# Context mixing of a two-layer decoder: from two programs over the whole stage to one program by batches

## The chip, the cores and the metric

The kernel runs on one core of a Trainium2 chip. The metric is device microseconds from launch to end, as the median of repeated runs. One further execution is recorded by the hardware profiler; all rows below are of that one.

## The reference

A decoder of two layers works on x, four batches of 512 tokens by 512 features. Each sublayer adds to x. The change lies in the second sublayer of layer 0, "context mixing", which follows an attention with 16 heads and stands ahead of a packed feed-forward net:

```
x = x + attention(layernorm(x))                      # layer 0 attention
x = x + context_mixing(layernorm(x), ctx, Wq, bq, Wk, bk)
x = x + packed_ffn(layernorm(x)); ...                # and layer 1

def context_mixing(xn, ctx, Wq, bq, Wk, bk):         # ctx: 4 x 512 x 256; Wq, Wk: 128 x 256
    query, key = ctx @ Wq.T + bq, ctx @ Wk.T + bk    # 4 x 512 x 128
    energy = query @ key.T                           # 4 x 512 x 512
    attention = softmax(energy)
    return xn @ attention.T                          # mixes the 512 features
```

The attention matrix depends on the context alone; x enters only in the last product.

## The kernel before, in words

x stays in on-chip memory as `x_res`, 16 tiles of 128 tokens by 512 features, 4 tiles to a batch. The decoder is a row of stages, each ended by a barrier of all engines. Every matrix product is made of three passes: each operand is split into a high and a low half (`_hi`, `_lo`), and high·high, high·low and low·high are summed. A tile that must lie the other way round is turned by TensorE (four 128x128 transposes into one 512-column bank, below a "turn"). ScalarE then copies the high half out of the bank, and VectorE takes the low half, which frees the bank.

`layer0_attention` projects queries and keys, stores them to device memory, and then attends over 32 pairs of heads. SyncE's queue loads pair after pair (`att.loads`, six pairs ahead).

`feature_attention` is the stage of the change. It holds two programs, one after the other.

The first, `load_context` with `norm_to_features`, loads the context (2 MB), the two weights and the two biases in one wave, and TensorE waits for all of them. VectorE meanwhile makes the statistics of all 16 tiles of x (`bn_stats`, L158). Then 8 turns of context and 2 of weights follow, the chain of small operations L163 to L171 with a square root on ScalarE (L232), and 16 turns of normalised x, through a ring of four `xn` buffers, into `xT_hi` and `xT_lo` for all four batches.

The second is the mixing. The banks are two `work`, four of `energy` and two `turn`. By batch b: `project_qk` makes query and key (12 matmuls, L1107), ScalarE and VectorE split them (L1157, L1180), `energies` makes 4 x 3 matmuls (L1116), VectorE takes the row maxima (L1188), ScalarE the exponentials (L1162), VectorE inverts the sums and scales the rows (L1195, L1198), `turn_attention` turns the 4 tiles (L1126, L1170, L1212), and `mix` makes four groups of 12 matmuls (L1137), each added to x by VectorE (L1204). The order of the work of each engine is written out by hand. For batch b TensorE does turn_attention(b), project_qk(b+1), energies(b+1), mix(b), so the softmax of the next batch lies beside the mixing.

`Ring` and `Norm` exist already and serve layer 0's attention: `Ring` is a list of turns through a few banks (a turn waits until the low half was taken of the job that had its bank before), `Norm` makes the statistics, the root and the scaling for one group of tiles.

Of the kernel before, what the change touches and what calls it, by code (L numbers as in the profile page):

```python
# [16 lines left out]
P = 128  # L17
F32 = mybir.dt.float32
# [12 lines left out]
T = B * QT  # L31
# [48 lines left out]
def setup(st, x_in):  # L80
    st.x_in = x_in

# [692 lines left out]
def layer0_attention(st, Wq_w, Wq_b, Wk_w, Wk_b, Wv_w, Wv_b):  # L775
# [4 lines left out]
    k_dram = nc.dram_tensor("l0_k", (2, HD, TOK), F32).ap()  # L780
    with ExitStack() as stack:
# [3 lines left out]
        wT_hi = sb("l0_wT_hi", [P, KC, D + 2 * HD], F32R)  # L785
        wT_lo = sb("l0_wT_lo", [P, KC, D + 2 * HD], F32R)
# [32 lines left out]
        k_stored = st.sem("k_stored")  # L819
# [232 lines left out]
def feature_attention(st, ctx_in, Wq, bq, Wk, bk):  # L1052

# [3 lines left out]
    with ExitStack() as stack:  # L1057
        sb, ps = tensors(nc, stack)
        features(st, stack, "fa")
# [5 lines left out]
        with ExitStack() as loading:  # L1065
            sb2, _ = tensors(nc, loading)
            raw = sb2("fa_w", [P, 2, C], F32)
            loads = [(raw[:, 0, :], Wq), (raw[:, 1, :], Wk), (bias[:, 0:1], column(bq)), (bias[:, 1:2], column(bk))]
            jobs = [([raw[:, n, c * P:(c + 1) * P] for n in range(2)], wT_hi[:, c, :], wT_lo[:, c, :])
                    for c in range(CC)]  # L1070
# [4 lines left out]
        prob = sb("fa_prob", [P, QT, S], F32)  # L1075
# [6 lines left out]
        energy = ps("fa_energy", [P, QT, S])  # L1082
        turn = [ps(f"fa_turn{n}", [P, 512]) for n in range(2)]
        worked, work_read, hi_done, scored, nmax_ready, exp_done, rden_done, prob_ready, turned, att_hi, turn_read = \
            st.sems("worked", "work_read", "hi_done", "scored", "nmax_ready", "exp_done", "rden_done", "prob_ready",
                    "turned", "att_hi", "turn_read")

# [8 lines left out]
        with nc.Block() as block:  # L1096

            @block.tensor
            def _(pe):
                def project_qk(b):  # L1100
                    for n in range(2):
                        if b:
                            pe.wait_ge(work_read, qk_use(b, n) - 1)
                        m = 0
                        for c in range(CC):
                            for w, x in ((wT_hi, ctxT_hi), (wT_hi, ctxT_lo), (wT_lo, ctxT_hi)):
                                last = pe.matmul(work[n][:], w[:, c, n * P:(n + 1) * P], x[:, c, b * S:(b + 1) * S],  # L1107
                                                 start=(m == 0), stop=(m == 3 * CC - 1))
                                m += 1
                        last.then_inc(worked, 1)  # L1110

                def energies(b):
                    pe.wait_ge(work_read, qk_use(b, 1) + 1)
                    for q in range(QT):
                        for m, (qq, kk) in enumerate(((hi[0], hi[1]), (hi[0], lo[1]), (lo[0], hi[1]))):
                            last = pe.matmul(energy[:, q, :], qq[:, q * P:(q + 1) * P], kk[:], start=(m == 0),  # L1116
                                             stop=(m == 2))
                        last.then_inc(scored, 1)

                def turn_attention(b):  # L1120
                    pe.wait_ge(prob_ready, b + 1)
                    for k in range(QT):
                        if QT * b + k >= 2:
# [1453 lines left out]
```

## Time and profile before

| what | us |
|---|---|
| median of 3 runs (2779.58 to 2780.4) | 2779.88 |
| the profiled execution's own time | 2776.81 |
| its span, first to last instruction | 2775.1 |
| layer 0 attention ends at | 375.6 |
| last addition of the mixing starts at | 514.07 |

Over the span TensorE's matmuls are busy 2493.5 us (90%), its weight loads 1808.0 (65%), VectorE 1750.2 (63%), ScalarE 1199.2 (43%). TensorE's matmuls overlap their neighbours, so a busy share of 90% does not say that TensorE is at its peak. In a timeline, the first column is the start, the second the duration, and the bracket at the end says how long the engine sat idle ahead of the row and what released it. A row of busy time by stretches gives the stretch, its length, the busy time with the number of instructions of TensorE's matmuls (PE), its weight loads (PEld), VectorE (DVE), ScalarE (ACT) and GpSimd (POOL), then TensorE's granted clock as a share of full speed, the share of the DMA engines and GB/s. A group of instructions gives busy time, mean ns of one, then the idle time ahead of them.

### The profile page before, as it was taken

Reading aid. Unit: us, or ns where it says so; the run is one execution under the profiler, and the core shown is the slowest. Engines: PE = TensorE matmul, PEld = TensorE weight load, DVE = VectorE, ACT = ScalarE, POOL = GpSimd, SP = SyncE. Lnnn points to the kernel's source line nnn. Section 1 sums busy time; section 2 is a strip of 40 time slices with the busy share of each in tenths; the row PEclk is TensorE's granted clock in tenths of the full one; section 3 lists DMA queues with packets and bytes.
Section 4 is the critical chain, followed back from the end, with each engine's and each line's share of the span. In section 5 each row is a group of like instructions: output and inputs, shape, how many; then the busy total and the mean of one; then the engine's idle time right before and its main releaser. Section 6 shows DMA issues by size and latency. Waiting matters only on the chain. (4 is left out here: it accounts for less than half of the span.)

```text
span 2775.1 us, 39696 instructions
## 1 busy us (share of the span) xinstructions
PE 2493.5 (90%) x11524; PEld 1808.0 (65%) x11524; DVE 1750.2 (63%) x3675; ACT 1199.2 (43%) x2342; POOL 157.6 (6%) x263
## 2 busy tenths in 40 slices
PE   7999968679999939989999689999999999999579
PEld 5555536557777727744445567777777777777457
DVE  6677765567777572256664657666666666767643
ACT  3566643223333232246664244444444444444321
POOL 0000000000000000010003011010100101010000
PEclk9999989779999979989999899999999999999789
DMA  5422110000000023343330100000000000000101
GB/s 166 129 69 68 48 34 0 17 1 1 0 0 0 1 65 121 118 117 89 84 78 0 32 30 12 11 15 4 15 11 8 11 11 15 4 8 0 39 1 61
DMA packets 71459, 103.69 MB, mean 37 GB/s; under 512 B 14447, under 2 KB 27514, under 8 KB 71262
## 3 DMA queue, kind: packets, MB, share of 16 engines
q1 hardware_dynamic: 71390, 102.82, 12.5%
q8 instruction: 37, 0.61, 0.1%
q14 instruction: 32, 0.26, 0.0%
HBM read 72.90 MB, written 29.88 MB: 37 GB/s over the span
## 5 line engine op out<-in xcount | busy, mean ns | idle before, releaser
L2470 DVE SCALAR_TENSOR_TENSOR x_res<-xa_out_bank,xa_den,x_res 128x512 f32 (+1 forms) x256 | 191.4, 748 | 158.5 <-PE xa_out_bank L2110 158.5
L2379 ACT ACTIVATE xa_pT_hi<-xa_t_bank 128x512 fp32r<-128x512 f32 x256 | 149.7, 598 | 125.8 <-PE xa_t_bank L2247 125.8
L2390 ACT ACTIVATE xa_prob<-xa_prob,xa_nmax 128x512 f32<-128x512 f32 x256 | 182.7, 716 | 30.0 <-DVE xa_nmax L2452 30.0
L2110 PE MATMUL xa_out_bank<-xa_o_w,xa_o_hi 128*128 128x512 f32 x512 | 172.8, 419 | 24.3 <-DVE x_res L2470 22.9
L2434 DVE TENSOR_TENSOR xa_pT_lo<-xa_t_bank,xa_pT_hi 128x512 fp32r<-128x512 f32 x256 | 175.8, 687 | 23.3 <-ACT xa_pT_hi L2379 19.3
L2452 DVE CUSTOM_DVE_ANT_0 xa_prob<-xa_s_bank,xa_mask_bias 128x512 f32<-128x512 f32 x256 | 171.1, 687 | 19.9 <-PE xa_s_bank L2110 9.5
L1535 DVE TENSOR_TENSOR ffn_y<-ffn_y 128x512 f32<-128x512 f32 x176 | 120.4, 689 | 70.5 <-PE ffn_y L1355 68.3
L581 DVE TENSOR_REDUCE l1s_mx<-l1s_max_bank 128x1 f32<-128x512 f32 x256 | 156.2, 681 | 12.7 <-PE l1s_max_bank L443 12.6
L581 DVE TENSOR_REDUCE l0s_mx<-l0s_max_bank 128x1 f32<-128x512 f32 x256 | 156.0, 681 | 2.8 <-PE l0s_max_bank L443 2.7
L2247 PE MATMUL xa_t_bank<-ident,xa_prob 128*128 128x128 f32 x1024 | 150.6, 275 | 0.0
L2247 PEld LDWEIGHTS xa_t_bank<-ident,xa_prob 128*128 128x128 f32 x1024 | 121.1, 141 | 39.6 <-issue 18.1
L568 ACT ACTIVATE l1s_pT<-l1s_score_bank 128x512 f32<-128x512 f32 x256 | 139.8, 601 | 15.3 <-PE l1s_score_bank L462 14.0
L568 ACT ACTIVATE l0s_pT<-l0s_score_bank 128x512 f32<-128x512 f32 x256 | 138.9, 601 | 9.1 <-PE l0s_score_bank L462 8.5
L443 PE MATMUL l1s_max_bank<-l1s_k,l1s_q 96*128 96x512 f32 x256 | 118.7, 473 | 16.6 <-DMA l1s_k<-l_k 8.4
L2371 ACT ACTIVATE xa_q_hi<-xa_bank_a 128x512 fp32r<-128x512 f32 x64 | 38.4, 600 | 197.5 <-PE xa_bank_a L2220 197.5
L2110 PEld LDWEIGHTS xa_out_bank<-xa_o_w,xa_o_hi 128*128 128x128 f32 x512 | 84.9, 190 | 59.2 <-issue 44.4
L472 PE MATMUL l1s_o_bank<-l1s_pT,l1s_vs 128*64 128x512 f32 x512 | 118.4, 605 | 0.0
L472 PE MATMUL l0s_o_bank<-l0s_pT,l0s_vs 128*64 128x512 f32 x512 | 116.9, 598 | 0.0
L443 PE MATMUL l0s_max_bank<-l0s_k,l0s_q 96*128 96x512 f32 x256 | 114.4, 451 | 2.2 <-DVE l0s_mx L581 1.6
L2259 PE MATMUL xa_o_bank<-xa_pT_hi,xa_v_hi 128*128 128x512 f32 x256 | 108.7, 425 | 0.1
L2110 PE MATMUL xa_s_bank<-xa_k_hi,xa_q_hi 128*128 128x512 f32 x256 | 106.4, 416 | 2.3 <-DVE xa_q_lo L2434 2.0
L462 PE MATMUL l1s_score_bank<-l1s_q,l1s_k 98*128 98x512 f32 x256 | 103.1, 406 | 1.8 <-ACT l1s_pT L568 1.1
(418 smaller groups left out, 5981.1 us busy)
## 6 DMA issues: line engine op xcount, KB each, us to landing
l0s_q<-l_q SPq DMA_DIRECT2D x96, 128.0 KB, 2.4
l1s_q<-l_q SPq DMA_DIRECT2D x96, 128.0 KB, 3.2
l1s_k<-l_k SPq DMA_DIRECT2D x96, 128.0 KB, 3.4
l0s_k<-l_k SPq DMA_DIRECT2D x96, 64.0 KB, 2.4
x_res<-in_x_dram SPq DMA_DIRECT2D x4, 1024.0 KB, 9.9
l_q<-l_q_hi SPq DMA_DIRECT2D x16, 256.0 KB, 2.7
l_q<-l_q_lo SPq DMA_DIRECT2D x16, 256.0 KB, 3.3
l_q<-l1p_hi SPq DMA_DIRECT2D x16, 256.0 KB, 2.1
```

What stands on the lines that cost most here:

```text
L443: pe.matmul(self.max_bank[(2 * s + j) % 3][:], self.qs[s][0:self.STK, n, q * P:(q + 1) * P], self.ks[s][0:self.STK, n % self.KN, :], start ...
L472: last = pe.matmul(self.o_bank[self.W * n:self.W * (n + 1), :], self.vs[s % 2][:, kt, n, :], self.pT[:, n, kt, :], start=(kt == 0), stop=( ...
L568: act.activation(self.pT[:, n, kt, :], self.score_bank[(2 * s + k) % 3][:], ACT.Exp, scale=HD ** -0.5)\
L581: dve.tensor_reduce(self.mx[:, j // QT, j % QT:j % QT + 1], self.max_bank[(2 * s + j) % 3][:], AX.X, ALU.max)\
L1535: dve.tensor_tensor(yt, y_bank[t % 2][:], yt, ALU.add).then_inc(y_read, 1)
L2110: last = pe.matmul(bank, w, x, start=(m == 0), stop=(m == len(pairs) - 1))
L2247: last = pe.transpose(t_bank[kt % 2][:, q * P:(q + 1) * P], prob[:, q, kt * P:(kt + 1) * P], st.ident[:])
L2379: act.activation(pT_hi[:, kt % (QT - 1), :], t_bank[kt % 2][:], ACT.Copy).then_inc(pT_hi_done, 1)
L2390: act.activation(prob[:, q, :], prob[:, q, :], ACT.Exp, bias=nmax[:, q:q + 1], scale=-1.0, accum_out=den[:, r, 0, q:q + 1]).then_inc(exp_d ...
L2434: dve.tensor_tensor(lo, bank, hi.bitcast(F32), ALU.subtract).then_inc(lo_done, 1)
L2452: dve.tensor_tensor_reduce(prob[:, q, :], s_bank[q % 2][:], mask_bias[:], -scale, -LOW * 1e-5, ALU.add, ALU.min, nmax[:, q:q + 1]).then_in ...
L2470: dve.scalar_tensor_tensor(xt, out_bank[:], den[:, r, 2, q:q + 1], xt, ALU.mult, ALU.add)\
```

## The change

The two programs of `feature_attention` become one, by batches.

1. Context and weights are loaded by `layer0_attention` (now `project_and_attend`), on SyncE's queue behind the last stores of projections and ahead of `att.loads`, into the room of layer 0's projection weights. The biases are loaded in the mixing program.
2. All turns (weights, context, x, attention) go through one `Ring` with three banks. `energy` has three banks in place of four, `work` still two. The context of batch b+2 is turned in the middle of mix(b).
3. x is normalised by batches with `Norm`: statistics, root and scaling of batch b+1 lie beside the work of batch b. Its turned form exists for one batch at a time.
4. The scaling of the softmax's rows moves from VectorE to ScalarE, and `prob` has two buffers.

```
 layer 0 attention, SyncE
+                sp.wait_ge(projected, NF * B)
+                sp.dma_start(st.fa_raw[0], ctx_in.rearrange("b (q p) c -> p (b q) c", p=P)).then_inc(fa_loaded, 16)
+                for n, w in enumerate((fa_Wq, fa_Wk)):
+                    sp.dma_start(st.fa_raw[1][:, n, :], w).then_inc(fa_loaded, 16)
                 att.loads(sp)
+                sp.wait_ge(fa_loaded, 48)
...
-            load_context(st, ctx_in, ctxT_hi, ctxT_lo, loads, jobs, "fa_prep")
+        norm = Norm(st, stack, "fan", [t[:] for t in xn])
-        energy = ps("fa_energy", [P, QT, S])
-        turn = [ps(f"fa_turn{n}", [P, 512]) for n in range(2)]
+        energy = [ps(f"fa_energy{n}", [P, S]) for n in range(3)]
+        turn = [ps(f"fa_turn{n}", [P, 512]) for n in range(3)]
+        ring = Ring(st, "far", turn, jobs)
...
 TensorE
+                def energies(b, q):
+                    if q == 0:
+                        pe.wait_ge(work_read, qk_use(b, 1) + 1)
+                    reached(pe, exp_done, QT * b + q - 2)
...
-                project_qk(0)
-                energies(0)
+                for c in range(CC):
+                    ring.turn(pe, at["w", c])
+                turn_context(0)
+                for n in range(2):
+                    project_qk(0, n)
+                turn_context(1)
+                for q in range(QT):
+                    energies(0, q)
                 for b in range(B):
-                    turn_attention(b)
-                    if b < B - 1:
-                        project_qk(b + 1)
-                        energies(b + 1)
+                    more = b + 1 < B
+                    for q in range(3):
+                        turn_x(b, q)
+                    if more:
+                        project_qk(b + 1, 0)
+                    turn_x(b, 3)
+                    turn_attention(b, 0)
+                    if more:
+                        project_qk(b + 1, 1)
+                    turn_attention(b, 1)
+                    turn_attention(b, 2)
+                    if more:
+                        energies(b + 1, 0)
+                    turn_attention(b, 3)
+                    if more:
+                        for q in range(1, QT):
+                            energies(b + 1, q)
                     for t in range(QT):
                         mix(b, t)
+                        if t == 1 and b + 2 < B:
+                            turn_context(b + 2)
...
 ScalarE
+                norm.root(act, 0, batch_tiles(0))
+                for c in range(CC):
+                    ring.take_hi(act, at["w", c])
+                take_context(0)
+                for n in range(2):
+                    take_qk(0, n)
+                take_context(1)
                 exponentials(0)
+                normalise(0)
                 for b in range(B):
+                    more = b + 1 < B
+                    for q in range(3):
+                        ring.take_hi(act, at["x", b, q])
+                    if more:
+                        take_qk(b + 1, 0)
+                    ring.take_hi(act, at["x", b, 3])
+                    ring.take_hi(act, at["a", b, 0])
+                    if more:
+                        take_qk(b + 1, 1)
+                    for k in range(1, QT):
+                        ring.take_hi(act, at["a", b, k])
+                    if more:
+                        norm.root(act, b + 1, batch_tiles(b + 1))
                         exponentials(b + 1)
+                        normalise(b + 1)
+                    if b + 2 < B:
+                        take_context(b + 2)
...
 VectorE
+                norm.stats(dve, 0, batch_tiles(0))
...
                 maxima(0)
                 normalise(0)
+                invert(0)
                 for b in range(B):
...
+                    for k in range(1, QT):
+                        ring.take_lo(dve, at["a", b, k])
+                    if more:
+                        norm.stats(dve, b + 1, batch_tiles(b + 1))
                         maxima(b + 1)
+                        add(b, 0)
+                        invert(b + 1)
+                        add(b, 1)
+                        if b + 2 < B:
+                            take_context(b + 2)
                         normalise(b + 1)
+                        add(b, 2)
+                        add(b, 3)
```

In the new program `normalise` on VectorE scales x (`Norm.normalise`), and `normalise` on ScalarE scales the four rows of `prob`. VectorE's order in the part that is left out is ScalarE's: each low half follows its high half.

## Rows read from the trace of the kernel before

**Rows 1.** Busy time by stretches: the stage of the change.

```profile
375.70:515.90 140.20, 102.75 (x452) 81.00 (x452) 80.66 (x142) 43.49 (x85) 0.00 (x0) 0.87 0.06 17
```

**Rows 2.** Timeline of all engines, start of the stage and its last addition.

```profile
377.00 0.40 SPq L101 DMA_DIRECT2D fa_prep_ctx<-in_ctx_dram  x1
377.34 9.59 DVE L158 BATCH_NORM_STATS2 fa_prep_bn<-x_res  x16 [1.71 <-PEq L57]
386.54 6.16 PEld L117 LDWEIGHTS fa_prep_w_bank<-ident,fa_prep_ctx 128*128 128x128 f32 x32 [12.31 <-DMA fa_bias<-in_L_xattn_bk_dram]
...
514.07 0.69 DVE L1204 TENSOR_TENSOR x_res<-fa_work,x_res 128x512 f32<-128x512 f32 x1 [2.10 <-PE fa_work L1137]
```

**Rows 3.** Groups of instructions by line and shape, stretch 376 to 516.

```profile
L1162 ACT ACTIVATE fa_prob<-fa_energy,fa_nmax 128x512 f32<-128x512 f32 x16 | 10.8, 686 | 9.2 <-DVE fa_nmax L1188 9.2
L1212 DVE TENSOR_TENSOR fa_attT_lo<-fa_turn,fa_attT_hi 128x512 fp32r<-128x512 f32 x16 | 10.5, 688 | 6.2 <-ACT fa_attT_hi L1170 6.2
L1180 DVE SCALAR_TENSOR_TENSOR fa_lo<-fa_work,fa_bias,fa_hi 128x512 fp32r<-128x512 f32 x8 | 6.0, 752 | 10.6 <-ACT fa_hi L1157 10.6
L1157 ACT ACTIVATE fa_hi<-fa_work,fa_bias 128x512 fp32r<-128x512 f32 x8 | 5.5, 688 | 11.2 <-PE fa_work L1107 11.2
```

**Rows 4.** Busy time by stretches: turning part of batch 1, turning and mixing of batch 3.

```profile
453.00:463.10 10.10, 7.56 (x40) 5.84 (x39) 6.20 (x10) 4.37 (x9) 0.00 (x0) 1.00 0.00 0
496.20:501.00 4.80, 2.46 (x18) 1.72 (x16) 3.27 (x5) 2.28 (x4) 0.00 (x0) 1.00 0.00 0
501.00:514.80 13.80, 12.98 (x48) 10.08 (x48) 2.77 (x4) 0.00 (x0) 0.00 (x0) 0.88 0.00 0
```

**Rows 5.** Timeline of TensorE: first projection; batch 1's turns and first mixing matmul; batch 2's turns.

```profile
416.46 0.77 PE L1107 MATMUL fa_work<-fa_ctxT_hi,fa_wT_hi 128*128 128x512 f32 x1 [2.00 <-PEq L190]
...
453.00 1.04 PE L1126 MATMUL fa_turn<-ident,fa_prob 128*128 128x128 f32 x8
...
463.49 0.39 PE L1137 MATMUL fa_work<-fa_attT_hi,fa_xT_hi 128*128 128x512 f32 x1
...
474.68 1.03 PE L1126 MATMUL fa_turn<-ident,fa_prob 128*128 128x128 f32 x8
```

**Rows 6.** Busy time by stretches: after the first softmax's idle time.

```profile
425.40:429.00 3.60, 0.09 (x1) 0.09 (x2) 2.58 (x7) 1.54 (x6) 0.00 (x0) 1.00 0.00 0
429.00:431.00 2.00, 1.25 (x9) 0.85 (x9) 0.76 (x2) 1.19 (x2) 0.00 (x0) 0.66 0.00 0
```

**Rows 7.** Timeline of VectorE in layer 0's projection: statistics of one batch by `Norm`.

```profile
20.30 2.47 DVE L745 BATCH_NORM_STATS2 l0n_bn<-x_res 128x6 f32<-128x512 f32 x4
23.80 0.16 DVE L753 SCALAR_TENSOR_TENSOR l0n_mv<-l0n_mv 128x4 f32<-128x4 f32 x1
25.73 1.92 DVE L767 TENSOR_SCALAR l0s_pT<-x_res,l0n_mv 128x512 f32<-128x512 f32 x4
```

**Rows 8.** Timeline of ScalarE: table loads, in layer 0 and in the mixing.

```profile
73.55 1.28 ACT L970 ACT_TABLE_LOAD   x1
74.84 0.20 ACT L970 ACTIVATE l0s_warm<-ident 128x1 f32<-128x1 f32 x1
...
421.56 1.28 ACT L1162 ACT_TABLE_LOAD   x1
424.11 0.69 ACT L1162 ACTIVATE fa_prob<-fa_energy,fa_nmax 128x512 f32<-128x512 f32 x1 [1.27 <-DVE fa_nmax L1188]
```

**Rows 9.** Timeline of TensorE: batch 1's projections and first energy, at half clock.

```profile
432.60 0.78 PE L1107 MATMUL fa_work<-fa_ctxT_hi,fa_wT_hi 128*128 128x512 f32 x1
...
438.96 0.50 PE L1116 MATMUL fa_energy<-fa_hi 128*128 128x512 f32 x1 [1.56 <-DVE fa_lo L1180]
```

**Rows 10.** Groups of ScalarE's instructions: one that reads and writes on-chip memory.

```profile
L1428 ACT ACTIVATE ffn_h_hi<-ffn_h 128x512 fp32r<-128x512 f32 x44 | 27.8, 633 | 139.8 <-DVE ffn_h L1525 139.8
```

**Rows 11.** Timeline of SyncE's queue at the end of the projections.

```profile
94.25 0.43 SPq L850 DMA_DIRECT2D l_q<-l_q_lo  x1
102.82 0.38 SPq L416 DMA_DIRECT2D l0s_q<-l_q  x1
```

More of the change, by code:

```diff
@@ L780, in layer0_attention @@
     k_dram = nc.dram_tensor("l0_k", (2, HD, TOK), F32).ap()
+    NW = D + 2 * HD
+    st.carried = ExitStack()
+    with ExitStack() as under:
+        wT_hi, wT_lo = (sb_tensor(nc, under, f"l0_wT_{part}", [P, KC, NW], F32R) for part in ("hi", "lo"))
+    later = sb_tensor(nc, st.carried, "fa_raw", [P, 2 * KC * NW])
+    st.fa_raw = (later[:, 0:T * C].rearrange("p (t c) -> p t c", t=T),
+                 later[:, T * C:T * C + 2 * C].rearrange("p (n c) -> p n c", n=2))
+    ctx_in, fa_Wq, fa_Wk = st.fa_inputs
     with ExitStack() as stack:
@@ L1096, in feature_attention, with _ @@
         with nc.Block() as block:
+            @block.sync
+            def _(sp):
+                for n, vec in enumerate((bq, bk)):
+                    sp.dma_start(bias[:, n:n + 1], column(vec), allow_slow_non_contiguous=True).then_inc(b_loaded, 16)
+                sp.wait_ge(b_loaded, 32)
             @block.tensor
             def _(pe):
[L1100 to L1123, printed above, removed]
-                            pe.wait_ge(turn_read, QT * b + k - 1)
-                        for q in range(QT):
-                            last = pe.transpose(turn[k % 2][:, q * P:(q + 1) * P], prob[:, q, k * P:(k + 1) * P],
-                                                st.ident[:])
-                        last.then_inc(turned, 1)
+                def project_qk(b, n):
+                    u = qk_use(b, n)
+                    reached(pe, work_read, u - 1)
+                    pe.wait_ge(ring.lo_done, at["c", b, CC - 1] + 1)
+                    m = 0
+                    for c in range(CC):
+                        for w, x in ((wT_hi, ctxT_hi), (wT_hi, ctxT_lo), (wT_lo, ctxT_hi)):
+                            last = pe.matmul(work[n][:], w[:, c, n * P:(n + 1) * P], x[:, c, b * S:(b + 1) * S],
+                                             start=(m == 0), stop=(m == 3 * CC - 1))
+                            m += 1
+                    last.then_inc(worked, 1)
@@ new lines, in energies @@
+                def energies(b, q):
+                    if q == 0:
+                        pe.wait_ge(work_read, qk_use(b, 1) + 1)
+                    reached(pe, exp_done, QT * b + q - 2)
+                    for m, (qq, kk) in enumerate(((hi[0], hi[1]), (hi[0], lo[1]), (lo[0], hi[1]))):
+                        last = pe.matmul(energy[(QT * b + q) % 3][:], qq[:, q * P:(q + 1) * P], kk[:], start=(m == 0),
+                                         stop=(m == 2))
+                    last.then_inc(scored, 1)
@@ L1166, in _, with take_context @@
+                def take_context(b):
+                    for c in range(CC):
+                        ring.take_hi(act, at["c", b, c])
+                norm.root(act, 0, batch_tiles(0))
+                for c in range(CC):
+                    ring.take_hi(act, at["w", c])
[3 more added lines that the diff above has]
+                take_context(1)
                 exponentials(0)
+                normalise(0)
                 for b in range(B):
-                    for k in range(QT):
-                        act.wait_ge(turned, QT * b + k + 1)
-                        act.activation(attT_hi[:, k, :], turn[k % 2][:], ACT.Copy).then_inc(att_hi, 1)
```

150 lines of the change are left out of this document (97 added, 53 removed).

## The prediction

> **What bounds the kernel now.** I read the busy time by stretches first. The stage lasts 140.2 us, from 375.7 to 515.9; TensorE is busy 102.75 us of it at a mean granted clock of 0.87, VectorE 80.66, ScalarE 43.49 [rows 1]. No engine is full, so the order of the work sets the time.
>
> The timeline then shows two halves. VectorE starts at 377.34 with 16 statistics (9.59 us). TensorE waits 12.3 us, until 386.54, for the last of five loads issued from 377.00 on [rows 2]. Ten turns of context and weights, the chain with the root and 16 turns of x follow, until the first projection at 416.46 [rows 5]. From there one batch costs 21.7 us: the turns of batch 1 start at 453.00 and those of batch 2 at 474.68. Of this 48 mixing matmuls take 474.68 − 463.49 = 11.2 us, 0.233 each [rows 5]. The turning part ahead of them (attention turns, projections, energies) lasts 10.1 us with TensorE busy 7.56, at full clock [rows 4]. So the old stage is 39 us of preparation and start, and 98 us of batches and their ends.
>
> **The change part by part.** One turn costs TensorE 0.42 us (two last 1.04 with the tail of the last [rows 5]), at half clock 4 x 6.16/32 = 0.77 [rows 2]. The high half then costs ScalarE 0.60 and the low half VectorE 0.69 [rows 3]. A matmul's result comes 0.2 us behind its slot (it lasts 0.39 [rows 5]). Handing over between engines costs 0.03 to 0.06, which I put into the sums.
>
> *The loads.* The three move to SyncE's queue in layer 0. The last store ahead is issued at 94.25 and the first reload of a pair at 102.82 [rows 11]. Even if the queue were held for the whole 9.5 us that all five loads take [rows 2], the first reload would come at 104.2, 1.4 us late. It brings pair 6, needed four pairs on, at (375.6 − 100)/32 = 8.6 us a pair. Cost 0; the attention beside it is the cover. The biases are two issues at the new program's start, needed some 10 us later: 0.
>
> *The start, new.* 377.3: statistics of four tiles and their chain, 3.67 us (20.30 to 23.96 [rows 7]). The root is first on ScalarE's queue and holds the high halves behind it until 381.2. Two weight halves (each about 0.4) and the two contexts of batch 0, the second one waiting for a bank and turned at half clock: 384.7. Two projections to the first energy: 6.4 us, as 432.60 to 438.96 [rows 9], since TensorE sat nearly idle: 390.9. Four energies, maxima and exponentials: with three banks the fourth energy waits for the first exponential. First maximum at 392.0, first exponential 392.7 to 393.4, fourth energy until 394.3, its maximum until 395.05. VectorE then scales four tiles of x (two small ones and 1.92 [rows 7]) before it inverts the sums: 397.5. ScalarE scales four rows at 0.6 to 0.63 (the nearest row reads and writes on-chip memory in 0.633 [rows 10]): 400.0. Only then does it take the turned x.
>
> *One batch's turning part.* From the first turn of x, TensorE's order makes this chain: three turns 1.26, first projection 1.40, two turns 0.84, second projection 1.40 plus 0.2, ScalarE takes the key 0.69, VectorE 0.75 [rows 3], first energy at 6.6, last attention turn until 7.3, to ScalarE 0.63, high 0.60, low 0.69: 9.3 us. Eleven of VectorE's pieces fit in (7.7 us), as do ScalarE's (6.2).
>
> *The new stall.* After the last turn TensorE has energies 1 and 2, done at 9.15, and then energy 3, which wants the bank of energy 0, so its exponential. Behind energy 3 in the queue stands the whole mixing. VectorE's order puts the next batch's statistics ahead of its maxima: 9.3 + 3.67 = 13.0. ScalarE does the root (13.2) and must then load the exponential's table, 1.28 [rows 8]: 14.5; exponential 0.69: 15.2. Energy 3 takes 0.7, and mixing starts at 15.9. TensorE idles 6.1 us in each of three batches.
>
> *The mixing.* 11.2 us and two context turns 0.84: the batch ends at 28.0 at full clock, against 21.7 before. VectorE's additions, invert, context halves and scaling of x end before it (by my count at 27.2), so they cost nothing; if TensorE were 1 us faster here they would not either.
>
> *The clock.* In rows 6 TensorE goes idle at 425.4, and the granted clock, 1.00 until 429.0, is 0.50 soon after. My stall is longer, so the work behind it starts at half speed (1.2 GHz). What that costs shows at 501.0 to 514.8: clock 0.88 [rows 4], so 0.12 x 13.8 = 1.66 us. I take 1.65 for each batch. The last batch has no projections; its eight turns are a ring of three banks with 2.0 us a round, 0.67 each, 6.65 in all. TensorE is 50% busy there, as at 496.2 to 501.0 (2.46 of 4.8), after which the clock did fall: 1.65 again.
>
> **The sum.** Start to batch 0's mixing: 400.0, plus 8.65 (the turning part from ScalarE's first x on), plus 0.6 for a projection that I expect at half clock (full it is 0, wholly half 5), plus 6.6 for statistics to mixing: 415.9. Batch 0: 11.2 + 0.84 + 1.65 = 429.6. Batch 1: 28.0 + 1.65 = 459.2. Batch 2, without context turns: 28.8, 488.0. Batch 3: 6.65 + 11.2 + 1.65 and 0.9 for the last addition: 508.4. Before, that addition ends at 514.07 + 0.69 = 514.8 [rows 2]. The gain is 6.4 us: the profiled execution goes from 2776.8 to 2770.4. Its own time is 3.1 below the median shown, so against the median I say 2779.9 − 6.4 = 2773.5. The stages behind begin as before. Thus the wins (loads and most of the preparation, about 39 us up to the first projection) are nearly given back by four longer turning parts and three stalls.
>
> A rule that speaks against the change is that of the Trainium skill, "ScalarE: Activation LUTs", section "What ACT_TABLE_LOAD costs": a switch of table sets costs 2.66 us, 1.28 of load and 1.38 of drain. The trace does not bear out the second part: the load of 73.55 ends at 74.83 and the next activation starts at 74.84 [rows 8]. By the rule the sum would be some 1.38 worse at each of four exposed switches; it is rival C, priced below from a row.
>
> **The rivals.**
> A: the clock does not fall. For it: the whole turning part of batch 1 stayed at 1.00 with TensorE 75% busy [rows 4]. Against it: the 6.1 us without work. Four times 1.65 would come back, and the 0.6: 2766.3.
> B, the other side: the turning parts run at half clock. Turns were at 0.50 to 0.66 from 429 on [rows 6] and at 386 [rows 2]. The chain of 9.3 then becomes three turns 2.3, projection 2.6, two turns 1.5, projection 2.6 and tail 0.4, key 1.5, energy 1.3, turn 1.1, halves 1.3: 14.6, and energy 3 costs 0.6 more, 5.9 a batch. A single batch uses up 5.9 of the 6.4; from the second on the kernel is slower. All three: 2791. Against it: the part is 90% busy until the stall and follows a dense mixing.
> C: a table load has a drain behind it. For it: 1.27 us idle between the end of the load (422.84) and the exponential at 424.11 [rows 8]; against it: that exponential's maximum ended only just before, and 74.84. Four exposed switches at 1.27: 5.1, so 2778.6, no change that can be told.
> D: the hiding is worse than drawn: banks and handovers that come late in the start and at each batch, 1 us for each of four turning parts and 2 in the start, 2779.5. The context load would be part of it if it held up the pairs.
>
> **How the numbers follow.** Forecast 58 in 100, A 16, B 8, C 6, D 12. A measurement of this kernel tells 0.2% (5.6 us, 2774.3) from no change. The forecast's own range is 2770 to 2777; it lies at the border, so of its 58 I count 38 as faster and 20 as no change. Faster: 38 and A, 54. No change: 20, C and 11 of D, 37. Slower: B and 1 of D, 9. The range reaches from A to past D: 2765 to 2782.
>
> **What would show it.** After: no load at the stage's head, first turn's high half near 381.2, first mixing matmul near 416. TensorE idle about 6 us ahead of the fourth energy of batches 1 to 3, released by ScalarE's exponential, with a 1.28 us table load ahead of it. Mixing to mixing near 29 us. Granted clock half for some 3.5 us behind each stall. The last addition ends near 508. I am wrong if the mixing starts without that wait, if the clock stays at 1.00 (then 2766), if turns and projections ahead of the stall show half clock, or if layer 0's end moves from 375.6.

## The result, and the profile after

| | before | after |
|---|---|---|
| median, us | 2780.4 (20 runs, 2775.18 to 2785.11) | 2774.35 (20 runs, 2770.94 to 2777.44) |
| profiled execution, us | 2776.81 | 2776.7 |
| layer 0 attention ends at | 375.63 | 379.83 |
| first statistics of the stage start at | 377.34 | 381.26 |
| last addition of the mixing ends at | 514.76 | 512.85 |
| stage, statistics to last addition | 137.42 | 131.59 |

The changed kernel takes 0.9978 of the time before (95% interval 0.9971 to 0.9984), 6.05 us less. The forecast was 6.4 less, and 2773.5 us for the median. At 0.22% the gain lies just above the 0.2% that the prediction counts as told from no change, and its interval reaches down to 0.16%. The two profiled executions hardly differ, because the one of before lies at the low end of its runs and the one of after above its median. So the readings below compare lengths: the stage is 137.42 − 131.59 = 5.8 us shorter. "The stage" is always that stretch here, unless a start is named. All instants of the prediction shift by 381.26 − 377.34 = 3.92 us, and what is left is the error. The two ends of the stage, in VectorE's timeline, after:

```profile
381.26 2.47 DVE L749 BATCH_NORM_STATS2 fan_bn<-x_res 128x6 f32<-128x512 f32 x4 [1.43 <-PEq L57]
...
512.16 0.69 DVE L1305 TENSOR_TENSOR x_res<-fa_work,x_res 128x512 f32<-128x512 f32 x1 [2.12 <-PE fa_work L1188]
```

Busy time of the whole stage, after. The row answers to [rows 1]:

```profile
379.90:514.30 134.40, 98.89 (x452) 77.65 (x452) 75.30 (x150) 60.33 (x111) 0.00 (x0) 0.87 0.00 1
```

TensorE runs the same 452 matmuls at the same mean clock of 0.87, and it is still busy only 98.89 of 134.40 us. Its idle time was 140.20 − 102.75 = 37.5 us and is 35.5. The head of the stage with its loads and 16 turns of x is gone; the idle time has moved.

Timeline of all engines from the start to batch 0's softmax, after (rows left out between them):

```profile
384.96 0.21 ACT L762 ACTIVATE fan_mv<-fan_mv 128x4 f32<-128x4 f32 x1 [2.46 <-DVE fan_mv L757]
385.07 0.64 ACT L720 ACTIVATE fa_wT_hi<-fa_turn 128x256 fp32r<-128x256 f32 x2
...
388.48 0.79 PE L1154 MATMUL fa_work<-fa_ctxT_hi,fa_wT_hi 128*128 128x512 f32 x1 [1.41 <-DVE fa_ctxT_lo L725]
...
394.79 0.50 PE L1164 MATMUL fa_energy<-fa_hi 128*128 128x512 f32 x1 [0.76 <-DVE fa_lo L1280]
...
399.41 1.91 DVE L771 TENSOR_SCALAR fa_xn<-x_res,fan_mv 128x512 f32<-128x512 f32 x4
...
401.44 2.57 ACT L1241 ACTIVATE fa_prob<-fa_prob,fa_rden 128x512 f32<-128x512 f32 x4 [1.53 <-DVE fa_rden L1293]
...
405.36 0.75 PE L709 MATMUL fa_turn<-ident,fa_xn 128*128 128x128 f32 x4 [2.39 <-DVE fa_xT_lo L725]
```

The root stands first on ScalarE's queue, and the high half of the first weights follows it at 385.07, though TensorE had turned the weights from 381.26 on. ScalarE scales four rows in 2.57 us, and the first turned x is taken only behind that. The fourth turn of x waits 2.39 us for the bank that this holds.

Timeline of all engines around the first stall, after:

```profile
413.07 1.28 ACT L762 ACT_TABLE_LOAD   x1
413.08 0.69 DVE L725 TENSOR_TENSOR fa_attT_lo<-fa_turn,fa_attT_hi 128x512 fp32r<-128x512 f32 x1 [0.93 <-ACT fa_attT_hi L720]
413.69 2.46 DVE L749 BATCH_NORM_STATS2 fan_bn<-x_res 128x6 f32<-128x512 f32 x4
...
417.18 0.16 DVE L757 SCALAR_TENSOR_TENSOR fan_mv<-fan_mv 128x4 f32<-128x4 f32 x1
417.27 1.89 DVE L1287 TENSOR_REDUCE fa_nmax<-fa_energy 128x1 f32<-128x512 f32 x3
417.38 0.21 ACT L762 ACTIVATE fan_mv<-fan_mv 128x4 f32<-128x4 f32 x1 [3.02 <-DVE fan_mv L757]
417.60 1.28 ACT L1235 ACT_TABLE_LOAD   x1
418.90 0.69 ACT L1235 ACTIVATE fa_prob<-fa_energy,fa_nmax 128x512 f32<-128x512 f32 x1
...
419.73 0.79 PE L1164 MATMUL fa_energy<-fa_hi 128*128 128x512 f32 x1 [5.92 <-ACT fa_prob L1235]
```

This is the chain that the prediction drew. Statistics (3.65 us), root, table load and exponential lie one behind another, while three finished energies wait for their maxima and TensorE waits for a bank. The exponential starts 418.90 − 417.60 − 1.28 = 0.02 us behind the end of its table's load.

The waits of TensorE in the stage (380 to 514), after: us in total, times, the longest. The row shown is the largest:

```profile
PE fa_energy L1164 <- ACT fa_prob L1235: 18.0, 4, 5.9
```

Busy time by stretches across that stall, after. They answer to [rows 6]; the clock is the third figure from the end:

```profile
413.00:415.00 2.00, 0.81 (x4) 0.33 (x2) 1.92 (x4) 1.34 (x2) 0.00 (x0) 1.00 0.00 0
415.00:417.00 2.00, 0.00 (x0) 0.00 (x0) 1.83 (x7) 0.00 (x0) 0.00 (x0) 0.74 0.00 0
417.00:419.00 2.00, 0.00 (x0) 0.00 (x0) 1.97 (x5) 1.59 (x3) 0.00 (x0) 0.50 0.00 0
...
421.00:425.00 4.00, 4.00 (x15) 3.13 (x15) 0.77 (x2) 0.80 (x3) 0.00 (x0) 0.78 0.01 4
```

The clock falls to 0.50 (1.2 GHz) while TensorE is idle, and the fourth energy and the first mixing matmuls run at that level. A turning part stays at 1.00 throughout (434 to 445, with TensorE busy 8.81 of 11 us, and 464 to 475 at 1.00 too).

Timeline of TensorE, after: the first turns of batches 1, 2 and 3, and batch 3's first mixing matmul. They answer to [rows 5]:

```profile
434.03 1.47 PE L709 MATMUL fa_turn<-ident,fa_xn 128*128 128x128 f32 x12
...
464.20 1.47 PE L709 MATMUL fa_turn<-ident,fa_xn 128*128 128x128 f32 x12
...
493.75 1.47 PE L709 MATMUL fa_turn<-ident,fa_xn 128*128 128x128 f32 x12
...
500.63 0.50 PE L1188 MATMUL fa_work<-fa_attT_hi,fa_xT_hi 128*128 128x512 f32 x1 [1.41 <-DVE fa_attT_lo L725]
```

From these, the stage against the prediction's sum:

| term | predicted | measured |
|---|---|---|
| start to the end of batch 0's mixing | 429.6 − 377.3 = 52.3 | 434.03 − 381.26 = 52.8 |
| batch 1 | 29.6 | 464.20 − 434.03 = 30.2 |
| batch 2 | 28.8 | 493.75 − 464.20 = 29.55 |
| batch 3, to the last addition's end | 20.4 | 512.85 − 493.75 = 19.1 |
| stage | 131.1 | 131.6 |

### The profile page after: what moved, and what is told of

It is laid out like the page before. It is cut to its first block and busy times, and to the rows that moved or that the text cites. A ratio compares the mean times of both kernels' runs of the same rounds, so it can differ in the third digit from the quotient of the medians.

```text
span 2775.0 us, 39683 instructions
## 1 busy us (share of the span) xinstructions
PE 2494.6 (90%) x11524; PEld 1807.2 (65%) x11524; DVE 1742.8 (63%) x3683; ACT 1218.0 (44%) x2367; POOL 157.4 (6%) x263
## 3 DMA queue, kind: packets, MB, share of 16 engines
q1 hardware_dynamic: 71390, 102.82, 12.5%
## 5 line engine op out<-in xcount | busy, mean ns | idle before, releaser
L2236 PE MATMUL xa_out_bank<-xa_o_w,xa_o_hi 128*128 128x512 f32 x512 | 173.3, 420 | 22.4 <-DVE x_res L2596 20.9
L572 ACT ACTIVATE l0s_pT<-l0s_score_bank 128x512 f32<-128x512 f32 x256 | 139.1, 603 | 10.9 <-PE l0s_score_bank L466 9.7
L2236 PE MATMUL xa_s_bank<-xa_k_hi,xa_q_hi 128*128 128x512 f32 x256 | 106.3, 415 | 2.2 <-DVE xa_q_lo L2560 2.0
```

The costliest lines, as they stand in the source:

```text
L572: act.activation(self.pT[:, n, kt, :], self.score_bank[(2 * s + k) % 3][:], ACT.Exp, scale=HD ** -0.5)\
L2236: last = pe.matmul(bank, w, x, start=(m == 0), stop=(m == len(pairs) - 1))
```

## The experiments

The stages of several experiments are compared in their profiles, since the executions of one kernel spread over 6.5 us (the changed one) to 9.9 us (the one before). Each median stands beside that of the kernel before, run on the same chip at the same time. Where an experiment ran beside the changed kernel too, that is said. Otherwise the two are compared by what each is below the kernel before, and that is 6.05 and 7.41 us for the changed kernel in its two series.

**The changed kernel again.** No edit.

> The changed kernel once more, for a second profile beside the variants. Theory: the stage (first instruction of the mixing program to the end of its last addition) again lasts 131.6 us, with three stalls of 5.9 us ahead of the fourth energy. Of layer 0's attention, which ended 4.2 us later in the one profile of after than in that of before (379.8 against 375.6) with a granted clock of 0.5 to 0.66 between 98 and 106 us: theory 1, the clock falls there by chance, so this profile can show either end; rival, the context load beside it brings it about, so it ends near 379.8 or at least 2.6 us late again.

Measured: 2774.7 us (10 runs) against 2782.11, ratio 0.997 (0.996 to 0.9979). The stage lasts 131.2 us. Layer 0's attention ends at 380.87, late again, so this run alone doesn't tell the theory from its rival; the next two do.

**The loads back into the stage.** Only part 1 of the change is undone (the lines are shortened):

```
 layer 0 attention, SyncE
-                sp.dma_start(st.fa_raw[0], ctx_in...)      # and Wq, Wk
                 att.loads(sp)
-                sp.wait_ge(fa_loaded, 48)
 mixing program, SyncE, ahead of the biases
+                sp.dma_start(ctx_raw, fa_in...)            # and Wq, Wk
 TensorE, ahead of the first turn
+                pe.wait_ge(fa_loaded, 48)
```

> The loads of context and weights go back into the mixing program, ahead of all else, with TensorE waiting for the three. Everything else stays as in the changed kernel. Theory: TensorE's first turn comes some 9.5 us after the issue instead of at once, of which 3.9 were covered by the first statistics: 6.3 us slower than the changed kernel, about the time of before. Rival, the load beside the attention costs 2.6 us or more there (see after_again): then the attention ends at 375.6 and only 3.7 us are lost.

Measured: 2782.51 us (10 runs), ratio 0.9996 (0.9986 to 1.0006) against the kernel before; 7.8 us above the changed kernel beside it. The stage is 138.27 us, 6.7 to 7.1 longer. It starts at 382.04, and TensorE's first turn waits for the last of the loads:

```profile
391.06 2.82 PE L709 MATMUL fa_turn<-ident,fa_raw 128*128 128x128 f32 x12 [11.60 <-DMA fa_raw<-in_L_xattn_Wk_dram]
```

The first projection comes 395.29 − 382.04 = 13.25 us behind the start in place of 7.22. So in this program the early load is worth as much as the whole gain, and the other three parts without it leave the time where it was. What an early load alone would give the kernel before was not run.

The experiment also bears on the test that the prediction failed: "if layer 0's end moves from 375.6". It did move, to 379.83. If the 2 MB beside the attention caused that, this kernel, which doesn't load them there, should end it at 375.6. It ends at 380.62.

**The kernel before, once more.** No edit, one execution.

> The kernel before once more, for a second profile. Eight profiles of variants show layer 0's attention ending between 376.7 and 380.9 with clock dips near 98 us and near 372 us, with the context load beside it or without; only the one profile of before shows 375.6 and no dip. Theory 1 (chance of the clock): this profile may show a dip as well, and in any case its stage from the end of the attention to the last addition lasts 139.1 us again, within 1. Rival (something of the changed kernel other than the load slows the attention): it ends at 375.6 again, without a dip.

Measured: 2784.46 us. Layer 0's attention ends at 378.70, 3.1 us later than in the first profile of the same kernel. From that end to the last addition it is 139.4 us (139.1 in the first profile). Busy time and granted clock near the start of the attention, in the order first profile of before, after, before once more, loads back:

```profile
97.00:105.00 8.00, 7.59 (x34) 3.67 (x36) 6.62 (x14) 5.73 (x10) 0.00 (x0) 1.00 0.07 26
```

```profile
97.00:105.00 8.00, 7.72 (x23) 4.73 (x24) 6.84 (x14) 4.48 (x8) 0.00 (x0) 0.60 0.77 250
```

```profile
97.00:105.00 8.00, 8.00 (x26) 5.51 (x28) 6.73 (x14) 5.08 (x9) 0.00 (x0) 0.62 0.01 2
```

```profile
97.00:105.00 8.00, 7.54 (x21) 4.60 (x21) 6.88 (x14) 4.11 (x7) 0.00 (x0) 0.64 0.07 26
```

The last three have the dip at 97 to 105, with 250 GB/s of loads or with 2 to 26. In the first profile of before the clock is 1.00 there. So the late end needs no load beside the attention. Nor does the load force it: in the nine profiles of kernels that have it there, the attention ends anywhere from 376.3 to 380.9. What is left is the clock, whose dips differ between executions of one kernel. That they make the end late is argued from their coming together, since no run forces a dip.

SyncE's queue in the changed kernel, which answers to [rows 11]:

```profile
94.47 0.43 SPq L860 DMA_DIRECT2D l_q<-l_q_lo  x1
97.78 0.39 SPq L871 DMA_DIRECT2D fa_raw<-in_ctx_dram  x1
98.22 3.05 SPq L873 DMA_DIRECT2D fa_raw<-in_L_xattn_Wq_dram  x1
101.32 0.49 SPq L873 DMA_DIRECT2D fa_raw<-in_L_xattn_Wk_dram  x1
105.08 0.37 SPq L420 DMA_DIRECT2D l0s_q<-l_q  x1
```

The three issues hold the queue until 101.8. The first reload comes at 105.08, 2.3 us later than before. But it stands 0.54 us behind the start of the first pair's output product (104.54), as it did before (102.82 behind 102.28) and does with the loads put back (105.63 behind 105.10). So it waited for the pair and not for the queue. The profile shows no wait of TensorE for a transfer during the whole attention.

**The stall filled with matmuls, in two amounts.** To price the clock apart from the wait, the third energy of batches 1 to 3 is computed N times over, 3 matmuls each time. The work fills idle time and moves nothing else:

```
-                    for m, (qq, kk) in enumerate(...):
-                        last = pe.matmul(energy[...][:], ...)
+                    for again in range(N if b and q == 2 else 1):
+                        for m, (qq, kk) in enumerate(...):
+                            last = pe.matmul(energy[...][:], ...)
```

N = 6:

> The third energy of batches 1 to 3 is computed six times over on the same operands instead of once, 5 x 0.70 = 3.5 us of idle TensorE filled per stall, nothing taken away. My term of the clock: the stall is idle for 2.5 us instead of 5.9, the clock stays at full speed, and each of three mixings saves 1.65 us: 5.0 us faster than the changed kernel. Rival (the slow start of the mixing has another cause than the idle time, or the 1.65 is covered): no change, or slower if the repeats delay the maxima.

N = 9:

> As e_warm, but the third energy is computed nine times over, which fills 5.6 of the 5.9 us of a stall and leaves TensorE about 0.4 us idle ahead of the fourth energy. In e_warm 2.5 us were left idle, the clock still fell in it, and only 0.3 us a batch came back. Theory (the clock falls because of the idle time ahead of the mixing): the fourth energy and the mixing now run at full clock from their start, 1.65 us saved in each of three batches less what the repeats delay: 4 to 5 us faster than the changed kernel. Rival (repeats of the same product do not count, or the drop has another cause): within 1.5 us of e_warm.

Measured, N = 6: 2773.46 us (5 runs), 1.2 under the changed kernel beside it, and no difference that can be told; 5.0 were expected. N = 9: 2768.27 us (4 runs), ratio 0.9949 (0.9932 to 0.9965); the changed kernel stood at 0.9978 and 0.997. Its stage is 126.09 us, 5.1 to 5.5 less, where 4 to 5 were expected. Busy time by stretches across the first stall, and then TensorE's timeline at its end, N = 6:

```profile
417.00:419.00 2.00, 0.00 (x0) 0.00 (x0) 1.54 (x3) 1.99 (x4) 0.00 (x0) 0.89 0.00 0
419.00:421.00 2.00, 1.89 (x5) 1.51 (x6) 0.21 (x1) 1.39 (x5) 0.00 (x0) 0.50 0.03 8
```

```profile
419.11 0.79 PE L1165 MATMUL fa_energy<-fa_hi 128*128 128x512 f32 x1 [2.51 <-ACT fa_prob L1236]
```

and both for N = 9:

```profile
417.00:419.00 2.00, 1.51 (x8) 0.93 (x7) 0.93 (x2) 1.99 (x6) 0.00 (x0) 1.00 0.00 0
419.00:421.00 2.00, 2.00 (x10) 1.64 (x9) 0.69 (x1) 1.48 (x5) 0.00 (x0) 1.00 0.04 8
```

```profile
418.41 0.50 PE L1165 MATMUL fa_energy<-fa_hi 128*128 128x512 f32 x1 [0.48 <-ACT fa_prob L1236]
```

With 2.51 us left idle the clock fell all the same, and the first matmul behind it took 0.79 us. In the next two stalls of that kernel the fourth energy still ran at full speed and the clock fell to 0.50 just behind it. With 0.48 left it stayed at 1.00 and the matmul took 0.50. In the second case the second batch takes 28.33 us in place of 30.2. From the fourth energy to the next batch's first turn the changed kernel takes 14.30, 14.76 and 14.12 us in the three batches with a stall, and this one 12.91, 12.93 and 12.03. So the clock's price is 1.4, 1.8 and 2.1 us, 5.3 in all. The 6-fold case failed as a test of that price, because it didn't keep the clock; the expectation had taken for granted that it would. The other 5.9 us of each stall stay in both kernels, as the exponential comes no sooner.

**The fourth energy behind half of the mixing.** The instruction that waits for the bank is put where TensorE has independent work ahead of it. VectorE's order follows:

```
 TensorE
-                        for q in range(1, QT):
+                        for q in range(1, QT - 1):
                             energies(b + 1, q)
                     for t in range(QT):
                         mix(b, t)
+                        if t == 1 and more:
+                            energies(b + 1, QT - 1)
 VectorE
-                        maxima(b + 1)
+                        maxima(b + 1, range(QT - 1))
                         add(b, 0)
+                        maxima(b + 1, range(QT - 1, QT))
+                        add(b, 1)
                         invert(b + 1)
-                        add(b, 1)
-                        if b + 2 < B:
-                            take_context(b + 2)
                         normalise(b + 1)
                         add(b, 2)
+                        if b + 2 < B:
+                            take_context(b + 2)
                         add(b, 3)
```

> The fourth energy of the next batch moves behind the second mixing group, VectorE takes its maximum behind the first addition. My account of the batch (9.3 turning, 6.6 from statistics to mixing, 12.0 mixing, 1.65 clock) says that mixing then starts at 9.35 and a batch lasts 22.5 instead of 29.6 to 30.2: three times 7.1 to 7.6, 21 to 23 us faster than the changed kernel. Rival: statistics, maxima and table load bound the batch on VectorE and ScalarE anyway (the next batch's maxima come late, and the next turning part waits for them); then a third of that or less, under 8 us.

Measured: 2749.89 us (4 runs), ratio 0.9884 (0.9868 to 0.9901), 24.8 below the changed kernel beside it. The stage lasts 109.23 us, 22.0 to 22.4 less, and a batch 22.66; 21 to 23 less was expected. The other 2.4 us or more of the medians' difference lie outside the stage and were not traced. Timeline of all engines at the same place, and busy time of the stretch:

```profile
414.06 1.89 DVE L1289 TENSOR_REDUCE fa_nmax<-fa_energy 128x1 f32<-128x512 f32 x3
...
414.40 1.28 ACT L1237 ACT_TABLE_LOAD   x1
...
415.87 0.68 DVE L1307 TENSOR_TENSOR x_res<-fa_work,x_res 128x512 f32<-128x512 f32 x1
...
416.53 0.50 PE L1164 MATMUL fa_energy<-fa_hi 128*128 128x512 f32 x1
```

```profile
413.00:425.00 12.00, 11.97 (x61) 9.63 (x61) 9.57 (x23) 8.47 (x18) 0.00 (x0) 1.00 0.01 1
```

Statistics, root and table load are as long as before. But TensorE is mixing beside them: the fourth energy has no idle time ahead of it, TensorE is busy 11.97 of 12 us, and the clock stays at 1.00. The waits of TensorE for `fa_prob` fall from 18.0 us to 0.3. The stalls and their clock made 3 x 5.9 + 5.3 = 23 us, which is near the 22 found. A fourth bank for `energy` would be another cure; it was not tried.

**Statistics and root one batch ahead.** TensorE's order is left as it is, and the work between the last energy and the exponential is taken away:

```
 VectorE, batch 1's statistics behind batch 0's softmax; in the loop
-                        norm.stats(dve, b + 1, batch_tiles(b + 1))
                         maxima(b + 1)
                         add(b, 0)
                         invert(b + 1)
+                        if b + 2 < B:
+                            norm.stats(dve, b + 2, batch_tiles(b + 2))
 ScalarE, batch 1's root behind normalise(0); in the loop
-                        norm.root(act, b + 1, batch_tiles(b + 1))
                         exponentials(b + 1)
                         normalise(b + 1)
                     if b + 2 < B:
                         take_context(b + 2)
+                        norm.root(act, b + 2, batch_tiles(b + 2))
```

> Statistics and root of x move one batch ahead (the statistics of batch b+2 behind the inversion of batch b+1, their root behind the context's high halves); nothing else is moved, the fourth energy stays ahead of the mixing. By my account the stall is 3.67 of statistics, 0.25 of root, 1.28 of table load, 0.69 exponential: with the first two gone and the table load hidden behind VectorE's last low half, it shrinks from 5.9 to about 1.6 us, so 4.3 a batch and the clock's 1.65, three times, less 1.4 at the start where statistics 1 and their table load now hold up the first x: 13 to 17 us faster than the changed kernel. Rival (the table load is the stall's core, or the statistics push the additions behind the mixing): under 7 us.

Measured: 2757.02 us (4 runs), ratio 0.9909 (0.9893 to 0.9926). The stage lasts 115.08 us, 16.1 to 16.5 less, where 13 to 17 were expected. The median is 25.5 below the kernel before, so 18 to 19 better than the changed kernel. The table load and the fourth energy of batch 1:

```profile
414.51 1.28 ACT L1235 ACT_TABLE_LOAD   x1
415.85 0.69 ACT L1235 ACTIVATE fa_prob<-fa_energy,fa_nmax 128x512 f32<-128x512 f32 x1
...
416.68 0.50 PE L1164 MATMUL fa_energy<-fa_hi 128*128 128x512 f32 x1 [1.43 <-ACT fa_prob L1235]
```

The stall is 1.43 us in place of 5.92, and the energy runs at full clock. So 4.5 us of each stall lay between ScalarE's last high half and the table load of the exponential: in the changed kernel that load waits for VectorE's last low half (413.08 on), the statistics (3.65) and the root (0.2), and starts 417.60 − 411.02 = 6.6 us behind the first energy. Here it starts 414.51 − 412.46 = 2.05 behind it. The start grew by 2.3 us (the first energy of batch 1 comes 32.1 us behind the start in place of 29.8). The parts add up: 3 x 4.5 + 5.3 − 2.3 = 16.5. This is the second, independent way to the same cause.

**Invert ahead of the scaling of x.** In the start VectorE inverts the sums ahead of scaling x, so that ScalarE comes free sooner:

```
                 maxima(0)
-                normalise(0)
                 invert(0)
+                normalise(0)
```

> One swap at the start: VectorE inverts the sums of batch 0 before it scales x, not behind it. ScalarE's scaling of the four rows then starts when the last exponential is done, some 1.4 us sooner, and the first high half of x with it. Theory: 1.0 to 1.5 us faster than the changed kernel, all of it ahead of the first addition. Rival: the scaled x comes later by as much and the turns wait for it: no change.

Measured: 2769.96 us (4 runs, 2768.39 to 2775.28), ratio 0.9954 (0.9938 to 0.9971). By the median that is 5 to 6.5 us better than the changed kernel, more than the 1.0 to 1.5 expected; in the profile, whose own time of 2775.28 is the highest of the four, the stage is 133.47 us, 1.9 longer. Busy time of the same stretches in this kernel and, in the second fence, in the changed one:

```profile
400.00:403.00 3.00, 2.09 (x10) 2.10 (x11) 2.15 (x7) 2.96 (x6) 0.00 (x0) 0.53 0.01 3
403.00:407.00 4.00, 4.00 (x15) 3.31 (x14) 1.97 (x3) 1.84 (x4) 0.00 (x0) 0.50 0.00 0
```

```profile
400.00:403.00 3.00, 2.96 (x18) 2.28 (x18) 1.41 (x4) 1.56 (x3) 0.00 (x0) 1.00 0.01 3
403.00:407.00 4.00, 1.64 (x9) 1.50 (x10) 2.48 (x5) 3.63 (x7) 0.00 (x0) 0.84 0.00 0
```

ScalarE did take the first x sooner, by 0.5 us from the start (22.16 against 22.65), but in that execution the first turns and projections ran at 0.53 and 0.50. What the edit is worth by itself stays open; the three executions of 2768.4 to 2771.5 left no profile.

**All together.** Late fourth energy, invert first, and batch 0's statistics and root moved behind the first context and the first query:

```
 VectorE
-                norm.stats(dve, 0, batch_tiles(0))
                 for c in range(CC):
                     ring.take_lo(dve, at["w", c])
                 take_context(0)
+                norm.stats(dve, 0, batch_tiles(0))
 ScalarE
-                norm.root(act, 0, batch_tiles(0))
...
                 for n in range(2):
                     take_qk(0, n)
+                    if n == 0:
+                        norm.root(act, 0, batch_tiles(0))
```

> e_late and e_invert together, and at the start the root of batch 0 behind ScalarE's first query instead of ahead of all high halves, with its statistics behind VectorE's low halves of the first context (TensorE's order is that of e_late). By rows of after the high halves of the weights wait from 381.3 to 385.1 for statistics and root, 3.7 us. Sum of the parts: 22 to 25 (e_late), 1.4, and 3.7: 27 to 30 us faster than the changed kernel. Rival: the root's table load and the statistics only move the wait to the first query or the first energy: then 25, as e_late with e_invert.

and the same kernel again:

> e_best once more, since its four executions held one that stands far apart from the rest. Theory: median 2745 to 2750, 27 us under the changed kernel and some 34 under before, stage from the end of the attention to the last addition 106.3 us within 1.

Measured: 2745.95 us against 2782.49, ratio 0.9868 (0.9849 to 0.9888), and 2746.92 (2742.15 to 2748.1) against 2780.79, ratio 0.9876 (0.9859 to 0.9892). One of the first four executions took 9384.61 us; median and ratio leave it out (with it the median is 2747.91), the next four showed nothing of the kind, and its cause is not known. Since the first statistics have moved, the length is taken from layer 0's end to the last addition's: 139.1 before, 133.0 changed, 110.7 with the fourth energy late, 106.3 and 107.7 here. Busy time over that stretch, first of the two:

```profile
380.80:487.10 106.30, 93.95 (x452) 74.01 (x452) 75.08 (x151) 59.96 (x110) 0.00 (x0) 0.95 0.00 1
```

TensorE's 452 matmuls now fill 88% of the stretch at a clock of 0.95. The two medians lie 36.5 and 33.9 us below the kernel before, where the late fourth energy alone is 32.2. So the two edits at the start (invert first, root and statistics moved) gave 3.0 to 4.4 us in the profiles and 1.7 to 4.3 in the medians, together, where 1.4 + 3.7 was expected; no run parts them. The energy behind the mixing remains most of the gain. Against the changed kernel the medians give 26.5 to 30.5 us and the profiles 25.3 to 26.7, where 27 to 30 was expected. The second profile's 107.7 misses its expected 106.3 within 1. The difference lies wholly in the last batch, where in this one, of ten profiles with the same last batch, the clock fell at the start of the mixing:

```profile
470.50:473.00 2.50, 2.50 (x7) 1.92 (x8) 0.00 (x0) 0.00 (x0) 0.00 (x0) 0.50 0.00 0
```

## Why the prediction was right, and where its sizes were off

**The mechanism.** It held at each step but the clock in the last batch. Of 39 us ahead of the first projection 7.2 are left. What lies behind it grew from 98.3 to 124.4 us, by longer turning parts and a stall of 5.92, 5.93 and 5.92 us ahead of the fourth energy. Predicted were 6.1 us in each of three batches, released by ScalarE's exponential with the table load ahead of it. That the stall is caused by the order of work, and not by the amount, is shown twice: with the fourth energy behind half of the mixing the same work costs 22 us less, with the statistics a batch ahead 16 us less.

**The loads.** "Cost 0" is borne out by the kernel that puts them back: its attention ends no sooner. What the early load is worth (6.7 to 7.1 us) is as much as the whole gain: with the loads back the kernel is at 0.9996. The prediction weighed only the sum and has no such division.

**The sum.** It came within 0.5 us (131.1 against 131.6), and that is in part luck: the start and the two full batches were 0.5, 0.5 and 0.75 us too long, and the last batch was 1.3 too short. The 2770.4 for the profiled execution was missed by 6.3 us: the stage began 3.9 late and was 0.5 longer than predicted, and some 1.8 us lie behind it, where the prediction has the stages begin as before. What lies behind was not traced.
- Up to the first x that ScalarE takes, the error is 0: 400.0 + 3.92 is 403.92, and the row stands at 403.91. The root, the first projection (7.2 us behind the start, predicted 7.4) and the first energy (13.5, predicted 13.6) lie where they were put.
- "0.6 for a projection that I expect at half clock" was too little: 403.91 to the fourth energy took 15.8 us, predicted 15.15. The second projection ran nearly wholly at half clock (407 to 409 at 0.50), which by my estimate costs some 1.2 (six matmuls at 0.43 us in place of 0.23).
- The turning part was right: from the first turn of x to the first energy 440.71 − 434.03 = 6.7 us, predicted 6.6.
- The clock's price was 1.4, 1.8 and 2.1 us (from the N = 9 kernel), predicted 1.65 each: right on average, 0.4 us short in the three together. In batch 1 the fourth energy comes 449.44 − 434.03 = 15.4 us behind the first turn, predicted 15.2. The energy, the mixing and the context turns take 12.93 at full clock in the N = 9 kernel, where the sum has 0.7 + 12.04 = 12.74. With the clock's 1.84 that makes the 30.17 measured.
- The last batch lost nothing: the clock stayed at 1.00 to the end, where I had put 1.65 by [rows 4]. That stretch had TensorE busy 2.46 of 4.8 us; here it was 4.27 of 6.6 (494 to 500.6). Whether this made the difference was not tried. The second profile of all together has 4.14 of 6.5 us there (464 to 470.5), and in it the clock did fall to 0.50 behind. The other nine profiles with this last batch stayed at 1.00; both of the kernel before fell. So the prediction's clock for this batch failed in the changed kernel, and by chance that error cancels most of the others.

**The rivals.** A fell: the clock was at 0.50 behind all three stalls. Its price of 1.65 a batch was near for three of its four batches (5.3 us in all by the N = 9 kernel); the fourth lost nothing. B fell: the turning parts of batches 1 to 3 ran at 1.00; in batch 0's only the second projection was at 0.50. C fell: at the stalls the exponential starts 0.02 us behind the end of its table's load, with its maximum ready. The rule of the Trainium skill, "ScalarE: Activation LUTs", section "What ACT_TABLE_LOAD costs", puts 1.38 us of drain beside the load of 1.28. This trace agrees with the load and not with the drain. D fell: late banks and handovers explain at most 0.2 us a batch, and the 0.5 of the start is the half clock of its projection, far from 6 in all.

**The tests.** The first high half (385.07, less 3.92) came at 381.15 as named. The first mixing matmul, near 416 by the prediction, came at 421.18 − 3.92 = 417.3: the fourth energy was 0.7 late and itself ran at half clock. Half clock lasted 3.1, 4.1 and 4.5 us behind the stalls, in place of some 3.5. Mixing to mixing was 30 in place of 29; the last addition, moved by the later start, came 0.5 us late. "Layer 0's end stays" was a bad test, since the same kernel of before ends it at 375.6 or 378.7.

## What to carry to other kernels

- With a ring of banks one shorter than the group that fills it, the last of the group waits for the first one's consumer. What stands behind it in the engine's program waits as well, here the whole mixing for 5.9 us. Put that instruction behind work that needs neither; here this gave four times as much as the whole change.
- Between the last product of a group and the first softmax step that frees a bank, VectorE and ScalarE should have nothing else in their queues; a root there also cost a table load of 1.28 us on the way back.
- Undo each part of a large change by itself: here the program without one simple part (the earlier load) gained nothing. And compare lengths of stages, not two profiled executions' totals: these two differed by 0.1 us where the medians differ by 6.

## What the runs showed of the hardware

- The granted clock in a stretch that the change does not touch differs from execution to execution: 1.00 in one profile and 0.50 to 0.71 in the other eleven at 97 to 105 us. Layer 0's attention ended between 375.6 and 380.9 us in the profiles here. That spread is nearly as large as what the change is worth.
- Filling part of an idle gap brought little of the clock back here. With 3.4 us of matmuls in a gap of 5.9 (2.5 left idle) it fell to 0.50 as in the empty one, and the stretch behind was 0.1 us shorter in the first stall and 0.3 in the second; with 5.4 us (0.5 left) it stayed at 1.00 and that stretch was 1.4 to 2.1 us shorter. In the kernel with the statistics ahead a gap of 1.43 us left it at 1.00.
- ScalarE's scaling of a 128x512 tile within on-chip memory took 713 ns (mean of 16), 2.57 us for four in a row, against 0.6 to 0.63 assumed from the 633 ns of [rows 10]. The pitch of 0.64 made the assumption nearly right.
